# The sixteen-head local attention network: from four-tile rounds to one pipeline over all tiles, with P·V computed transposed

## The chip, the cores and the metric

The kernel runs on one core of a Trainium2 chip. A time is the device time of one execution in microseconds (us). The kernel before took 2250.7, 2259.16 and 2259.73 us in three runs, median 2259.16 us.

## The reference

Two layers run one after the other on x of shape (4, 512, 128): four batches of 512 tokens with 128 features.

```python
x = L0_attn_x
xn = layernorm(x)
s = L0_attn(xn)                 # retention over chunks, 4 heads
g = silu(L0_ffn(xn))            # the network of depth 6, below
x = x + s * g
xn = layernorm(x)
s = L1_attn(xn)                 # one head of masked attention
g = silu(L1_ffn(xn))            # 8 experts, top 2
x = x + s * g
```

The change touches `L0_ffn` alone. Its reference, cut to what matters:

```python
for i in range(6):
    x = attn_layer(shift_tokens(x), Wqkv[i], q_scale[i], k_scale[i], Wo[i]) + x
    x = ffn_layer(shift_tokens(x), ln_g[i], ln_b[i], W1[i], b1[i], W2[i], b2[i]) + x
# attn_layer, 16 heads of 64, windows of 32 tokens:
q, k, v = split(x @ Wqkv)                     # 128 -> 3 * 1024
q, k = l2norm(q) * qs, l2norm(k) * ks         # then rotary, with a scale by position
sim = 8 * q . k  over the own window of 32 and the one before it, masked
out = softmax(sim) @ v, then out @ Wo         # 1024 -> 128
# ffn_layer: layernorm, xn @ W1 + b1 -> a, gate (341 each), a * gelu(gate) @ W2 + b2
```

All is float32.

## The kernel before, in words

Three builders run one after the other: `build_retention`, `build_network` (this is `L0_ffn`, and all that changes) and `build_second_layer`. The features of x lie on the partitions, `state[128, 4 x 516]`.

The network has 6 layers x 4 batches = 24 rounds, and a round has 4 tiles of 128 tokens (96 tiles). For each tile the work is this:

- TensorE projects q and k into `qk_ps` (4 banks, `project_qk` L393) and v into the ring (`project_v` L380). The ring is 2 PSUM banks used in turn by everything that isn't q, k or the scores; before it writes a bank, TensorE waits for the reader of the fill two places earlier (`bank_free`).
- VectorE multiplies q and k by the rotary tables (`rotate` L708, L713; the half `k` after ScalarE's squares), GpSimd adds the two products (L352). ScalarE squares q and k (L575), VectorE sums by head (L721), ScalarE takes Ln and Exp (L580, L584), VectorE makes one Newton step (L733 to L737), and GpSimd multiplies by the inverse norms (L359).
- TensorE transposes q and k (`transpose_qk` L404), ScalarE copies them to SBUF (the helper at L564 makes all such copies). The scores are 64 small matmuls per tile (L423), after two that write the mask (L418), into the two banks `sc_ps`.
- VectorE takes the row maximum (L742), subtracts it (L747), ScalarE exponentiates (L613), VectorE sums the rows (L755) and takes the reciprocal; TensorE transposes exp(S) (L438), ScalarE copies, and TensorE multiplies by the windows of v (`attend` L453) into the same `sc_ps`. VectorE multiplies the product by 1/sum (`normalise` L767), TensorE transposes it (`transpose_o` L467) and ScalarE copies it to `oT`.
- SyncE moves v from token order into windows with 16 DMAs a tile (`move_windows`, L293 and L296).

A tile takes three stages: projections in its own, scores one later, softmax and P·V two later. Once a round come the output projection (L475, 8 matmuls of 512 columns), the LayerNorm (L481, L486), the gated network (L493, L495, `gelu` L603, L789) and its second matrix (L502, L796), all for the round before. The orders are written out by hand for each engine (`pe_round`, `act_round`, `dve_round`): stages s=0 and s=1 of a round hold only tile work, s=2 also the whole output projection and the LayerNorm, s=3 also the whole feed-forward part. Each engine executes its own list strictly in order.

`ident`, `ones` and mask constants are made first. At a layer's first round GpSimd rebuilds the rotary tables `rot` (L341), after VectorE has finished with the old ones.

## Time and profile before

| | before |
|---|---|
| median of 3 runs | 2259.16 us |
| the profiled execution: its own time | 2256.97 us |
| its span, from the first to the last instruction | 2255.2 us |
| mean granted TensorE clock | 0.972 |
| matmul instructions on TensorE | 31016 |
| DMA, q1 | 120.64 MB in 83600 packets |

An instruction line of a list by lines reads: line, engine, operation, output<-input, count | busy us in all, mean ns of one | idle time of the engine just before them and what ended it. PE is TensorE, PEld its weight loads, DVE VectorE, ACT ScalarE, POOL GpSimd, SP SyncE. A float32 matmul appears as two MATMUL instructions, a float32 transpose as one. In a timeline the first number is the start, the second the length of the merged piece, which runs to the modelled end of the last matmul; the distance between two starts tells what a piece costs a busy TensorE.

### The profile page before, as it was taken

The page shows a single profiled execution, that of the slowest core. Times are in us where ns is not written, and L with a number is a line of the kernel's source. Part 1 is how long each engine was busy: PE and PEld are TensorE (multiplying, and loading weights), DVE is VectorE, ACT ScalarE, POOL GpSimd, SP SyncE. Part 2 cuts the span into 40 slices and gives each one's busy share as a digit, 9 for nine tenths or more (in the row PEclk, how much of TensorE's full clock was granted, in tenths as well). Part 3 has the DMA queues.
Part 4 walks back from the last instruction along what each step waited for, and adds up shares of the span by engine and source line. Part 5 has one row for each costly group of instructions (what it writes and reads, how often), then busy time and mean ns, then how long its engine had stood idle before and what let it go on. Part 6 is the DMA issues. An engine that isn't in the chain of part 4 may idle for free. (4 is left out here: it accounts for less than half of the span.)

```text
span 2255.2 us, 71087 instructions
## 1 busy us (share of the span) xinstructions
PE 1958.2 (87%) x31016; PEld 1121.9 (50%) x31016; DVE 1561.8 (69%) x2095; ACT 1151.2 (51%) x1934; POOL 863.9 (38%) x427
## 2 busy tenths in 40 slices
PE   6858889889989898989889898899988888986898
PEld 5635455455545544554555454455544545543444
DVE  6648777777767877777777777778777777863443
ACT  4425555554655555455555555555555555553234
POOL 0225444444434534444443444444445444430000
PEclk9979999999999999999999999999999999997788
DMA  1023222223222322222232222232223222221000
GB/s 42 1 72 93 48 54 60 73 58 75 54 46 56 87 66 58 55 51 67 62 79 50 57 57 74 49 75 62 50 56 86 66 49 56 60 52 43 0 9 10
DMA packets 83885, 124.96 MB, mean 55 GB/s; under 512 B 26112, under 2 KB 31880, under 8 KB 82704
## 3 DMA queue, kind: packets, MB, share of 16 engines
q1 hardware_dynamic: 83600, 120.64, 22.2%
q8 instruction: 242, 3.96, 0.8%
q14 instruction: 43, 0.35, 0.1%
HBM read 21.98 MB, written 1.05 MB: 10 GB/s over the span
## 5 line engine op out<-in xcount | busy, mean ns | idle before, releaser
L352 POOL TENSOR_TENSOR t<-t 128x1024 f32<-128x1024 f32 x192 | 453.3, 2361 | 661.4 <-DVE t L713 661.4
L359 POOL TENSOR_TENSOR qkn<-t,rn 128x1024 f32<-128x1024 f32 x192 | 374.2, 1969 | 373.9 <-DVE rn L737 373.9
L393 PE MATMUL qk_ps<-wqkv,state 128*128 128x512 f32 x768 | 396.5, 599 | 11.5 <-DMA wqkv<-in_w_qkv 9.2
L708 DVE TENSOR_TENSOR t<-qk_ps,rot 128x1024 f32<-128x1024 f32 x192 | 234.5, 1222 | 195.4 <-ACT sq L575 135.5
L404 PEld LDWEIGHTS ring<-ident,qkn 128*128 128x128 f32 x1536 | 180.9, 141 | 198.9 <-issue 122.0
L404 PE MATMUL ring<-ident,qkn 128*128 128x128 f32 x1536 | 233.8, 278 | 26.2 <-POOL qkn L359 25.6
L713 DVE TENSOR_TENSOR t<-qk_ps,rot 128x1024 f32<-128x1024 f32 x192 | 233.1, 1214 | 0.0
L721 DVE TENSOR_REDUCE lnsum<-sq 128x16 f32<-128x1024 f32 x192 | 231.8, 1208 | 0.0
L564 ACT COPY prT<-ring 128x512 f32<-128x512 f32 x192 | 113.2, 590 | 217.2 <-PE ring L438 217.2
L575 ACT ACTIVATE sq<-qk_ps 128x1024 f32<-128x1024 f32 x192 | 198.0, 1031 | 39.0 <-PE qk_ps L393 38.0
L564 ACT COPY oT<-ring 128x512 f32<-128x512 f32 x192 | 112.6, 586 | 184.0 <-PE ring L467 184.0
L380 PE MATMUL ring<-wqkv,state 128*128 128x512 f32 x384 | 200.4, 624 | 3.6 <-DMA wqkv<-in_w_qkv 2.7
L423 PE MATMUL sc_ps<-kT,qT 64*32 64x64 f32 x12288 | 170.6, 224 | 23.9 <-issue 23.9
L423 PEld LDWEIGHTS sc_ps<-kT,qT 64*32 64x32 f32 x12288 | 135.9, 105 | 83.1 <-issue 82.8
L475 PE MATMUL ring<-oT,wo 128*128 128x512 f32 x384 | 170.7, 598 | 0.7 <-ACT oT L564 0.7
L453 PE MATMUL sc_ps<-v_win,prT 64*32 64x64 f32 x12288 | 168.1, 225 | 2.7 <-issue 1.6
L564 ACT COPY v_tok<-ring 128x512 f32<-128x512 f32 x192 | 112.1, 584 | 113.3 <-PE ring L380 113.3
L453 PEld LDWEIGHTS sc_ps<-v_win,prT 64*32 64x32 f32 x12288 | 135.6, 106 | 63.9 <-issue 62.3
L564 ACT COPY qT<-ring 128x512 f32<-128x512 f32 x192 | 111.4, 580 | 104.7 <-PE ring L404 104.7
L742 DVE TENSOR_REDUCE smax<-sc_ps 128x16 f32<-128x1024 f32 x96 | 117.2, 1221 | 68.1 <-PE sc_ps L423 68.1
L438 PE MATMUL ring<-ident,pexp 128*128 128x128 f32 x768 | 120.0, 279 | 29.5 <-ACT pexp L613 20.4
L438 PEld LDWEIGHTS ring<-ident,pexp 128*128 128x128 f32 x768 | 87.8, 140 | 111.0 <-issue 74.7
(235 smaller groups left out, 2727.2 us busy)
## 6 DMA issues: line engine op xcount, KB each, us to landing
v_win<-v_tok SPq DMA_DIRECT2D x1488, 64.0 KB, 2.0
wqkv<-in_w_qkv SPq DMA_DIRECT2D x6, 1024.0 KB, 5.6
wqkv<-in_w_qkv SPq DMA_DIRECT2D x6, 512.0 KB, 3.7
wo<-in_w_o SPq DMA_DIRECT2D x6, 512.0 KB, 3.8
w<-in_w SPq DMA_DIRECT2D x6, 341.0 KB, 4.0
w<-in_w SPq DMA_DIRECT2D x6, 192.0 KB, 3.9
r_xtok<-in_x SPq DMA_DIRECT2D x4, 256.0 KB, 4.0
amask<-in_att_mask SPq DMA_DIRECT2D x1, 1024.0 KB
```

Source lines behind the costliest of these rows:

```text
L352: nc.gpsimd.tensor_tensor(t1[:, to], t1[:, to], t2[:, to], ALU.add).then_inc(qk_added.sem, 1)
L359: nc.gpsimd.tensor_tensor(qkn[:, to].rearrange("p (h d) -> p h d", d=DH), t1[:, to].rearrange("p (h d) -> p h d", d=DH), rn[:, HEADS * hal ...
L380: nc.tensor.matmul(to, tile_of(r, s), wqkv[:, 2 * INNER + 512 * par:2 * INNER + 512 * (par + 1)], start=True, stop=True).then_inc(v_full.s ...
L393: nc.tensor.matmul(qk_ps[:, c, :], tile_of(r, s), wqkv[:, 512 * c:512 * (c + 1)], start=True, stop=True).then_inc(qk_full.sem, 1)
L404: ins = nc.tensor.transpose(to[:, n * P:(n + 1) * P], qkn[:, c * P:(c + 1) * P], ident[:, :])
L423: ins = nc.tensor.matmul(sc_ps[WIN * q:WIN * (q + 1), par, 64 * pair:64 * (pair + 1)], qT[64 * par:64 * (par + 1), pair, WIN * q:WIN * (q ...
L438: ins = nc.tensor.transpose(to[:, n * P:(n + 1) * P], pe_[:, c * P:(c + 1) * P], ident[:, :])
L453: ins = nc.tensor.matmul(sc_ps[WIN * q:WIN * (q + 1), par, DH * pair:DH * (pair + 1)], prT[64 * par:64 * (par + 1), pair, WIN * q:WIN * (q ...
L564: nc.scalar.copy(to, bank_of(r, (what, s, lag, f))).then_inc(done.sem, 1)
L708: nc.vector.tensor_tensor(t1[:, to].rearrange("p (h d) -> p h d", d=DH), own, rot[:, 2 * half, s:s + 1, :].to_broadcast([P, HEADS, DH]), A ...
L713: nc.vector.tensor_tensor(t2[:, to].rearrange("p (h s d) -> p h s d", s=2, d=DH // 2), swapped, rot[:, 2 * half + 1, s:s + 1, :].to_broadc ...
L721: nc.vector.tensor_reduce(lnsum[:, HEADS * half:HEADS * (half + 1)], sq[:, INNER * half:INNER * (half + 1)].rearrange("p (h d) -> p h d", ...
```

## The change

The network is written anew as a single chain of 102 stages (96 tiles and 6 to run empty), in which stage g works on tile g (projections), g-1 (transposes of q and k, scores), g-2 (softmax, transposes of P) and g-3 (P·V). All loops are unrolled, GpSimd's and SyncE's too.

- **P·V transposed.** `attend` makes the windows of v the stationary operand (64 rows x 64 columns) and P the moving one (32 columns), so that the product comes out as `oT` needs it. It goes to the two ring banks, no longer to `sc_ps`, and ScalarE copies it (`copy_o`). The eight transposes of the product and `o_tok` are gone. v and P are ordered so that heads n and n+8 share a chunk.
- **P normalised on GpSimd.** 1/sum is multiplied into exp(S) before the transposes (`scale_p`, two instructions of 128x512), in place of VectorE's `normalise`.
- **GpSimd's order.** q and k are scaled in four quarters of 128x512 in place of two halves of 128x1024, a stage later than they are summed; then come `scale_p` of tile g-2 and the two additions of tile g. The tables of the next layer are made ahead, into a second buffer.
- **The order on VectorE.** A stage begins with the row maximum and, right behind it, the row sum of the same tile (before, the sum stood one stage later). The Newton step stays there, as a maximum and four instructions in place of a maximum and three. On ScalarE a third instruction (a Relu) stands ahead of Ln and Exp, which now come behind the copies of P.
- **The order on ScalarE.** A stage begins with exponential, copy of o, exponential, copy of o.
- **The round's parts are spread.** The output projection is cut in two halves of 256 columns, one in the stage s=1 and one in s=2 of the next round; the LayerNorm is in its s=3, the two matrices of the feed-forward part in s=0 and s=1 of the round after that.
- SyncE loads Wq and Wk in two transfers, Wo at the end of a layer's first round, W1 and W2 in its second round. The moves of v stay as they were.

The diff, cut to its core:

```diff
+def stage_fills(g):
+    now, turn, prob, att = (tile_there(g - n) for n in range(4))
+    up, down = round_at(g, 0, 2), round_at(g, 1, 2)
+    out_0, out_1, centre = round_at(g, 1, 1), round_at(g, 2, 1), round_at(g, 3, 1)
+    fills = []
+    fills += [("a", g - 3, f) for f in range(2)] * att
+    fills += [("xc", centre, 0)] * (centre is not None)
+    fills += [("t", g - 1, 0)] * turn
+    fills += [("w2", down, 0)] * (down is not None)
+    fills += [("t", g - 1, 1)] * turn
+    fills += [(k, up, 0) for k in ("gate", "lin")] * (up is not None)
+    fills += [("t", g - 1, 2)] * turn
+    fills += [("v", g, 0)] * now
+    fills += [(k, up, 1) for k in ("gate", "lin")] * (up is not None)
+    fills += [("t", g - 1, 3)] * turn
+    fills += [("wo", out_0, 0)] * (out_0 is not None)
+    fills += [("var", centre, 0)] * (centre is not None)
+    fills += [("v", g, 1)] * now
+    fills += [("wo", out_1, 1)] * (out_1 is not None)
+    fills += [(k, up, 2) for k in ("gate", "lin")] * (up is not None)
+    fills += [("p", g - 2, f) for f in range(2)] * prob
+    return fills
...
+    def scale_qk(g, f):
+        if f == 0:
+            pool.wait_ge(rn_ready, g + 1)
+        if f % 2 == 0:
+            added = (q_added, k_added)[f // 2]
+            pool.wait_ge(added, g + 1)
+        nc.gpsimd.tensor_tensor(by_head(quarter(qkn, f)), by_head(quarter(qkn, f)),
+                                rn[:, 8 * f:8 * (f + 1)].unsqueeze(2).to_broadcast([P, 8, DH]), ALU.mult).then_inc(qk_scaled, 1)
+    def add_terms(g, k):
+        turned = (q_rot, k_rot)[k]
+        pool.wait_ge(turned, 2 * (g + 1))
+        if g > 0:
+            pool.wait_ge(qkT_full, 4 * (g - 1) + 2 * (k + 1))
+        nc.gpsimd.tensor_tensor(half(qkn, k), half(t1, k), half(t2, k), ALU.add).then_inc((q_added, k_added)[k], 1)
+    def scale_p(g, f):
+        if f == 0:
+            pool.wait_ge(rden_ready, g + 1)
+            if g > 0:
+                pool.wait_ge(pT_full, 2 * g)
+        nc.gpsimd.tensor_tensor(by_head(quarter(pn, f)), by_head(quarter(pe_, f)),
+                                rden[:, 8 * f:8 * (f + 1)].unsqueeze(2).to_broadcast([P, 8, DH]), ALU.mult).then_inc(p_scaled, 1)
+    tables(0)
+    for g in range(TILE_COUNT + 2):
+        if tile_there(g - 1):
+            for f in range(4):
+                scale_qk(g - 1, f)
+        if tile_there(g - 2):
+            for f in range(2):
+                scale_p(g - 2, f)
+        if tile_there(g):
+            for k in range(2):
+                add_terms(g, k)
+        l = g // (B * TILES)
+        if g % (B * TILES) == 2 and l + 1 < DEPTH:
+            tables(l + 1)
...
+    def attend(g, f):
+        t = g % TILES
+        to = [bank_of("a", g, part) for part in range(2)]
         if f == 0:
+            pe.wait_ge(pT_copied, 2 * (g + 1))
+            pe.wait_ge(v_moved[t], moves_of[t] * (g // TILES + 1))
+            for part in range(2):
+                ring_bank("a", g, part)
+        for pair in range(2 * f, 2 * (f + 1)):
             for q in range(TW):
                 for par in range(2):
+                    n = 2 * pair + par
+                    for part in range(2):
+                        ins = nc.tensor.matmul(
+                            to[part][64 * par:64 * (par + 1), P * pair + WIN * q:P * pair + WIN * (q + 1)],
+                            v_win[64 * part:64 * (part + 1), TW * t + q, DH * n:DH * (n + 1)],
+                            prT[64 * part:64 * (part + 1), n, WIN * q:WIN * (q + 1)],
+                            start=True, stop=True)
         if f == 1:
+            ins.then_inc(av_full, 1)
...
+    for g in range(STAGES):
+        now, turn, prob, att = (tile_there(g - n) for n in range(4))
+        up, down = round_at(g, 0, 2), round_at(g, 1, 2)
+        out_0, out_1, centre = round_at(g, 1, 1), round_at(g, 2, 1), round_at(g, 3, 1)
+        for f in range(2):
+            if att:
+                attend(g - 3, f)
+            if now:
+                project_q(g, f)
+        if centre is not None:
+            ffn_centre(centre)
+        if turn:
+            transpose_qk(g - 1, 0)
+        if down is not None:
+            ffn_down(down)
+        if now:
+            project_k(g, 0)
+        if turn:
+            transpose_qk(g - 1, 1)
+        if now:
+            project_k(g, 1)
+        if up is not None:
+            ffn_up(up, 0)
+        if turn:
+            transpose_qk(g - 1, 2)
+        if now:
+            project_v(g, 0)
+        if up is not None:
+            ffn_up(up, 1)
+        if turn:
+            transpose_qk(g - 1, 3)
+        if out_0 is not None:
+            output_projection(out_0, 0)
+        if centre is not None:
+            ffn_variance(centre)
+        if now:
+            project_v(g, 1)
+        if out_1 is not None:
+            output_projection(out_1, 1)
+        if up is not None:
+            ffn_up(up, 2)
+        for f in range(2):
+            if prob:
+                transpose_p(g - 2, f)
+            if turn:
+                scores(g - 1, f)
...
+    def copy_o(g, f):
+        act.wait_ge(av_full, g + 1)
+        t = g % TILES
+        nc.scalar.copy(oT[:, 4 * f:4 * f + 4, P * t:P * (t + 1)], bank_of("a", g, f)).then_inc(oT_copied, 1)
+    def exponentials(g, f):
...
+    def inverse_norms(g):
+        act.wait_ge(sums_ready, 2 * (g + 1))
+        nc.scalar.activation(raised[:, :], sums[:, :], ACT.Relu, bias=low_col[:, 0:1]).then_inc(raised_ready, 1)
+        act.wait_ge(raised_ready, g + 1)
+        nc.scalar.activation(lnss[:, :], raised[:, :], ACT.Ln, scale=LN_SCALE, bias=low_col[:, 1:2]).then_inc(ln_ready, 1)
+        act.wait_ge(ln_ready, g + 1)
+        if g > 0:
+            act.wait_ge(rn_ready, g)
+        nc.scalar.activation(rs[:, :], lnss[:, :], ACT.Exp, scale=-0.5).then_inc(rs_ready, 1)
...
+    for g in range(STAGES):
+        now, turn, prob, att = (tile_there(g - n) for n in range(4))
+        up, centre = round_at(g, 0, 2), round_at(g, 3, 1)
+        for f in range(2):
+            if prob:
+                exponentials(g - 2, f)
+            if att:
+                copy_o(g - 3, f)
+        if centre is not None:
+            centred(centre)
+        for f in range(2):
+            if turn:
+                copy_qkT(g - 1, f)
+        if now:
+            squares(g, 1)
+        if up is not None:
+            gelu(up, 0)
+        if turn:
+            copy_qkT(g - 1, 2)
+        if now:
+            copy_v(g, 0)
+        if up is not None:
+            gelu(up, 1)
+        if turn:
+            copy_qkT(g - 1, 3)
+        if now:
+            squares(g, 0)
+        if centre is not None:
+            inverse_deviation(centre)
+        if now:
+            copy_v(g, 1)
+        if up is not None:
+            gelu(up, 2)
+            nc.scalar.preload_act_table_set(LN_EXP_SET)
+        for f in range(2):
+            if prob:
+                copy_pT(g - 2, f)
+        if now:
+            inverse_norms(g)
...
+    def row_sum(g):
+        dve.wait_ge(exp_ready, 2 * (g + 1))
+        nc.vector.tensor_reduce(den[:, :], by_head(pe_[:, :]), AX.X, ALU.add).then_inc(den_ready, 1)
+        dve.wait_ge(den_ready, g + 1)
+        if g > 0:
+            dve.wait_ge(p_scaled, 2 * g)
+        nc.vector.reciprocal(rden[:, :], den[:, :]).then_inc(rden_ready, 1)
...
+    def inverse_norms(g):
+        dve.wait_ge(sums_ready, 2 * (g + 1))
+        nc.vector.tensor_scalar(ss[:, :], sums[:, :], NORM_FLOOR, None, ALU.max).then_inc(newton, 1)
+        dve.wait_ge(rs_ready, g + 1)
+        nc.vector.tensor_tensor(nw1[:, :], rs[:, :], rs[:, :], ALU.mult).then_inc(newton, 1)
+        dve.wait_ge(newton, 4 * g + 2)
+        nc.vector.tensor_tensor(nw2[:, :], nw1[:, :], ss[:, :], ALU.mult).then_inc(newton, 1)
+        dve.wait_ge(newton, 4 * g + 3)
+        nc.vector.tensor_scalar(nw3[:, :], nw2[:, :], -0.5 * LN_SCALE * LN_SCALE ** 0.5, 1.5 * LN_SCALE ** 0.5, ALU.mult, ALU.add).then_inc(newton, 1)
+        dve.wait_ge(newton, 4 * g + 4)
+        if g > 0:
+            dve.wait_ge(qk_scaled, 4 * g)
+        nc.vector.tensor_tensor(rn[:, :], nw3[:, :], rs[:, :], ALU.mult).then_inc(rn_ready, 1)
...
+    def add_attention(r, f):
+        dve.wait_ge(wo_full, 2 * r + f + 1)
+        if f == 0 and r > 0:
+            dve.wait_ge(xc_full, r)
+            dve.wait_ge(x_ffn, 2 * r)
         for late, rows in enumerate(HALVES):
+            nc.vector.tensor_tensor(xa[rows, 2 * P * f + late:2 * P * (f + 1) + late], bank_of("wo", r, f)[rows, 0:2 * P],
+                                    state[rows, batch_cols(r, 2 * P * f + late, 2 * P)], ALU.add).then_inc(x_attn, 1)
...
+    for g in range(STAGES):
+        now, turn, prob, att = (tile_there(g - n) for n in range(4))
+        up, down = round_at(g, 0, 2), round_at(g, 1, 2)
+        out_0, out_1, centre = round_at(g, 1, 1), round_at(g, 2, 1), round_at(g, 3, 1)
+        if prob:
+            row_max(g - 2)
+            row_sum(g - 2)
+        if now:
+            rotate(g, 0)
+        if up is not None:
+            ffn_gated(up, 0)
+        if down is not None:
+            add_ffn(down)
+        if now:
+            rotate(g, 1)
+        if up is not None:
+            ffn_gated(up, 1)
+        if now:
+            sum_squares(g, 1)
+            sum_squares(g, 0)
+        if up is not None:
+            ffn_gated(up, 2)
+        if out_0 is not None:
+            add_attention(out_0, 0)
+        if out_1 is not None:
+            add_attention(out_1, 1)
+        if now:
+            inverse_norms(g)
+        if centre is not None:
+            ffn_norm(centre)
```

## Rows read from the trace of the kernel before

**Rows 1.** the page, part 1: busy us (share of the span) xinstructions

```profile
PE 1958.2 (87%) x31016; PEld 1121.9 (50%) x31016; DVE 1561.8 (69%) x2095; ACT 1151.2 (51%) x1934; POOL 863.9 (38%) x427
```

**Rows 2.** timeline of PE, a plain stage: start, us, engine, line, operation

```profile
1089.69 1.02 PE L393 MATMUL qk_ps<-wqkv,state 128*128 128x512 f32 x2 [0.86 <-issue]
1090.55 0.60 PE L404 MATMUL ring<-ident,qkn 128*128 128x128 f32 x4
...
1095.53 0.86 PE L453 MATMUL sc_ps<-v_win,prT 64*32 64x64 f32 x64
...
1101.14 0.59 PE L418 MATMUL sc_ps<-mask_bf,ident_bf 128*128 128x512 bf16 x2 [1.46 <-DVE o_tok L767]
...
1104.42 1.02 PE L393 MATMUL qk_ps<-wqkv,state 128*128 128x512 f32 x2
```

**Rows 3.** timeline of PE, the first projections of the network and of round 1

```profile
141.82 6.53 PE L393 MATMUL qk_ps<-wqkv,state 128*128 128x512 f32 x8 [9.23 <-DMA wqkv<-in_w_qkv]
...
201.59 1.02 PE L393 MATMUL qk_ps<-wqkv,state 128*128 128x512 f32 x2
```

**Rows 4.** timeline of PE, output projection, second matrix, start of the next round

```profile
1027.67 7.03 PE L475 MATMUL ring<-oT,wo 128*128 128x512 f32 x16
...
1067.26 2.82 PE L502 MATMUL ring<-gel,w 128*128 128x512 f32 x6
...
1152.80 1.02 PE L393 MATMUL qk_ps<-wqkv,state 128*128 128x512 f32 x2
```

**Rows 5.** timeline of PE, behind the last tile's scores

```profile
2023.27 0.60 PE L404 MATMUL ring<-ident,qkn 128*128 128x128 f32 x4
...
2039.34 2.05 PE L453 MATMUL sc_ps<-v_win,prT 64*32 64x64 f32 x128 [0.68 <-ACT prT L564]
```

**Rows 6.** PE in stretches: us, PE busy (x), PEclk, DMA share, GB/s

```profile
2039.30:2041.40 2.10, 2.05 (x128) 0.50 0.03 8
```

**Rows 7.** timeline of PE, 64 moving columns with full weights (retention)

```profile
93.48 3.68 PE L1061 MATMUL pd<-vsb,at 128*128 128x64 f32 x32
```

**Rows 8.** the last additions (L796): ns min/median/max, first to last start

```profile
L796 DVE SCALAR_TENSOR_TENSOR state<-ring,col,xa x48: 734/750/760, 278.2 to 2073.9; 64x512 f32<-64x512 f32 x48
```

**Rows 9.** GpSimd's product by the inverse norms, by its line

```profile
L359 POOL TENSOR_TENSOR qkn<-t,rn x192: 1899/1902/2284, 156.4 to 2022.5; 128x1024 f32<-128x1024 f32 x192
```

**Rows 10.** groups by line and shape

```profile
L767 DVE TENSOR_TENSOR o_tok<-sc_ps,rden 128x512 f32<-128x512 f32 x192 | 122.9, 682 | 5.1 <-PE sc_ps L453 4.8 <-issue 0.3
...
L564 ACT COPY oT<-ring 128x512 f32<-128x512 f32 x192 | 112.6, 586 | 184.0 <-PE ring L467 184.0
L613 ACT ACTIVATE pexp<-pr 128x512 f32<-128x512 f32 x192 | 112.6, 628 | 18.5 <-DVE pr L747 18.4
...
L783 DVE TENSOR_SCALAR xn<-xc,col 128x512 f32<-128x512 f32 x24 | 46.7, 1946 | 0.9
...
L341 POOL TENSOR_TENSOR rot<-rot_base,qks 128x256 f32<-128x256 f32 x24 | 16.7, 729 | 10.2 <-DMA qks<-in_qk_scale 10.2
...
L1694 DVE TENSOR_SCALAR apr<-aex,arden 128x512 f32<-128x512 f32 x16 | 7.8, 486 | 0.6
```

**Rows 11.** timeline of DVE, the start of a plain stage

```profile
1088.28 1.23 DVE L742 TENSOR_REDUCE smax<-sc_ps 128x16 f32<-128x1024 f32 x1 [0.41 <-PE sc_ps L423]
1089.54 1.29 DVE L747 TENSOR_TENSOR pr<-sc_ps,smax 128x512 f32<-128x512 f32 x2
```

**Rows 12.** timeline of ACT, squares and gelu of stage s=3

```profile
1058.30 1.05 ACT L575 ACTIVATE sq<-qk_ps 128x1024 f32<-128x1024 f32 x1
1059.37 1.28 ACT L603 ACT_TABLE_LOAD   x1
```

**Rows 13.** timeline of ACT and DVE, Ln to the Newton step

```profile
1022.67 0.23 ACT L580 ACTIVATE lnss<-ss 128x32 f32<-128x32 f32 x1 [2.07 <-DVE ss L726]
...
1023.65 0.19 DVE L737 SCALAR_TENSOR_TENSOR rn<-nw,rs 128x32 f32<-128x32 f32 x1
```

**Rows 14.** what SP waited for: us in total, times, longest us

```profile
SPq L293 <- ACT v_tok L564: 815.7, 96, 15.7
```

804 lines of the change are left out of this document (284 added, 520 removed).

## The prediction

> **What bounds the kernel now.** I read the engines' busy shares first [rows 1]: TensorE is busy for 87% of the span, and nothing else is above 69%, so the question is what TensorE waits for. The share is an average, so next come the stretches between rounds. The network starts its first projection at 141.8 and round 1 at 201.6 [rows 3]; the transposes behind the last scores of round 23 start at 2023.3 [rows 5], and the last addition to the state ends at 2074.6 (2073.9 and 0.75) [rows 8]. Round 0 is thus 59.8 us, 23 rounds take 1821.7, or 79.2 each, and the emptying 51. The other 322 us of the span are untouched code.
>
> Within a round I read TensorE's timeline. A plain stage (s=1) takes 14.7 us, and near its end TensorE stands 1.46 us at the mask matmul, until VectorE has normalised the product of P and V out of the banks that the scores need [rows 2]; with the tail of the matmul before, some 1.7 us are lost, and 13.0 are work. The two stages with round work, s=2 and s=3, take 48.4 us together (1104.42 to 1152.80) [rows 2, 4]. Four times 13.0 plus the round's own matmuls, some 17 (6.9 for the output projection and 2.7 for the second matrix by [rows 4], six up-matmuls and the two of the LayerNorm at 0.9), are 69 of the 79.2: ten microseconds a round are waits.
>
> **What the change takes from TensorE.** The transposes of the product go: two groups of four, 0.60 each with a tail [rows 2], about 1.0 us a stage. P·V has as many matmuls as before, 64 a tile and two instructions each, but 64 stationary columns for 32 and 32 moving ones for 64. Its price isn't in the trace. Now 64 instructions pass in 0.86 [rows 2]. At half clock [rows 6] 128 pass in 2.05 [rows 5], only a fifth more than two such pieces: so at full clock it isn't the array that sets their pace, and the array alone could go nearly twice as fast. Twice the weights then about fill the pace they have: I take 0.85 a half, 1.7 a tile. From the other side, 32 matmuls with 128 stationary and 64 moving columns pass in 3.68 us, 0.11 each [rows 7]; half the columns would be 0.055, or 7.0 us a tile one behind the other and 3.5 if the two halves of the partitions load side by side. Both are kept for the range, and so is 0.8 a tile, should the halved moving columns count. TensorE's own work is then 12.1 a plain stage and 65 to 66 a round.
>
> The Trainium skill ("TensorE: Matmul & The Clock Gate", LDWEIGHTS) speaks against the edit: it counts a load by its columns, at 1.2 columns a ns, so that 64 take 53 ns where 32 took 27. By it P·V would be 3.4 a tile with two loads side by side. The trace agrees for the full weights of the retention, and 32 columns two abreast would take the 0.86 of now; but if that rate falls with the array's clock, the half-clock piece would have taken 3.4 us and not 2.05.
>
> **What takes the old wait's place.** The scores no longer wait for VectorE's normalising; `sc_ps` is free. But in the new order I find another chain. Let a plain stage start at 0 on TensorE, when the scores of tile g-2 are done.
> - VectorE isn't there yet: ScalarE's Ln and Exp now stand behind the two copies of P, whose second transpose ends 0.9 before the stage does. The copy is 0.59 [rows 10], Relu, Ln and Exp 0.75 (0.23 and a gap each), and the Newton step 0.95, where now three instructions and two waits lead from 1022.67 to 1023.84 together with Ln and Exp [rows 13]. So the row maximum starts at 1.6.
> - It takes 1.26 to the first subtraction (0.68) [rows 11]; then the exponential (0.63) and, queued behind it, the first copy of o (0.59) [rows 10]: done at 4.8. Only then is the ring bank free for the first transpose of q. TensorE has by then done P·V and two projections, 3.4 by my price, and stands about 1.4. Even at 3.5 a tile for P·V it would lose only a further 0.4.
> - From there: four transposes at 0.45, two k and two v projections at 0.86 to 0.95, P and the scores (mask 0.5, two halves at 0.8), with one stop of 0.9 where ScalarE has the squares of k (1.05 [rows 12]) ahead of the copies. The stage closes at 14.1, against 14.7 now.
>
> VectorE has some 12 of work there: the row maximum, the subtractions [rows 11], seven more passes over 1024 elements of that length, the reciprocal and the Newton step. The change takes 1.4 from it with `normalise` (two of 0.682 [rows 10]) and adds 0.2 in the Newton step. Nothing is gained by that alone, since VectorE now waits for the exponentials (1.1) and the norms (0.7).
>
> GpSimd: four quarter products at 1.05 and two for P at 1.05, between half of 1.90 [rows 9] and what a line from 0.73 for 256 elements [rows 10] to 1.90 for 1024 gives for 512. That is 6.3 and the two additions' 4.7, 11.0 of 14.1. The reciprocal is there at 7, the two P quarters at 9.2, and TensorE asks for the first at 10.8: hidden, up to some 1.8 for a quarter.
>
> The moves of v: SyncE waited 815.7 us in 96 waits for the copies of v [rows 14], 8.5 a tile; the product reads the windows a stage later than now. Hidden, and the weight loads too. The tables made ahead save the table wait at layer boundaries, under 3 us each; this I leave in the average.
>
> **Stages with round work**, walked in the same way:
> - s=3 (LayerNorm): two more fills and a copy and a square on ScalarE ahead of the copies of q: 16.6. VectorE ends with the normalisation of x, behind the Newton step. The scaling there (L783) is 1.95 now, beside GpSimd's product of 1.90, though one of the same size and kind alone takes 0.49 [rows 9, 10]. It waited out the GpSimd instruction. Quarters make that about 1.1. VectorE comes to the next stage at 3.2.
> - s=0 (gate and linear, six fills): the first transpose of q is held to 6.4 by that lag; then each second fill waits for a gelu or for VectorE's product: the table load (1.28) and the first gelu behind the squares hold the third transpose by 2.3, the gated product the v projection, ScalarE's squares of q the last linear part. 22.9, where the matmuls are 17.9.
> - s=1 (second matrix, half the output projection): the third transpose waits 0.8 for VectorE's addition to the state, the first of P 0.2 for the half just projected: 20.5.
> - s=2 (the other half): 17.5.
>
> Together 77.5, and 0.4 for semaphores: 77.9 against 79.2. The time of a round hardly moves, since the two-bank ring and strict queues give the waits back in other places.
>
> The Trainium skill ("SBUF — State Buffer", "SBUF: two separate sides") says that GpSimd and VectorE hold one pair of ports by turns, also against a VectorE operation with two SBUF inputs. The 1.95 of L783 agrees. By it three of the four Newton instructions, with two such inputs each, could stand behind a GpSimd one. GpSimd waits for the Newton result itself at that point, so the sum would be the same, except where the second addition is late: then up to 2.4 a stage.
>
> **The sum**, against the profiled execution's 2257.0 (span 2255.2 and 1.8 around it; the median, 2259.2, is 0.1% above):
> - round 0: stages of 10, 13, 14 and 14 and no round work, 51 for 59.8: -9
> - round 1: 14.1, 17.7, 17.5 and 16.7, still without the feed-forward part, 66 for 79.2: -13
> - 22 rounds at -1.3: -29
> - emptying: six stages, 20.6 and 11 with work of tiles, then P·V, projection, LayerNorm and the two matrices with nothing beside them, 28: 60 for 51: +9
> - stops not seen in a walk (instruction supply: the 0.86 "issue" in [rows 2], which is in the 79.2): half a microsecond a round: +12
>
> 2257 - 30 = **2227 us**.
>
> **The rivals.**
> 1. Fewer waits: s=0 and s=1 come down to near the matmuls, because the queues drift apart less than in my walk. 65.5 of TensorE work a round allow it; the ten waits of now speak against. At 74 a round: 2227 - 22 x 3.9 = 2141.
> 2. Slower, by the ring: in s=0 some fourteen fills pass through two banks whose readers, ScalarE and VectorE, each have squares, sums or a table load ahead of the read. If each handover there and in s=1 costs 0.2 more than I count, that is 4 us more a round. For: in s=2 and s=3 now 5 of 48.4 us are lost in the same kind of handovers; against: this is already as much as my walk has. At 82 a round: 2227 + 22 x 4.1 = 2317. It decides the sign from 79.3 a round on.
> 3. The weight loads bound P·V: at 3.5 a tile about +1.3 a round, 2256; at 7.0, one behind the other, TensorE is 3.9 late at the transpose in three stages of four: +13 a round, 2515.
> 4. The change doesn't do what it says: P's normalising isn't off the path, because a quarter on GpSimd takes as long as a half does now, 1.9. Six of them put the first P quarter at 11.1, 0.3 late in three stages of four: +1 a round, 2249.
>
> **Chances.** Forecast 0.45, rival 1 0.20, rival 2 0.24, rival 3 0.08, rival 4 0.03. A change under 0.5% (11 us) can't be told from none. The forecast's own range, 2200 to 2255, gives 0.38 faster and 0.07 same; rival 3 gives 0.05 same and 0.03 slower, rival 4 0.03 same. Faster 0.58, same 0.15, slower 0.27. The range runs from a little under rival 1 to rival 2: 2130 to 2320.
>
> **What would show it.** TensorE's wait at the mask for VectorE gone; in its place one at the first transpose of q for ScalarE's copy of o, 1 to 1.5 us a stage and more in s=0; P·V 64 instructions in about 0.85; stages of 14, 17.5, 20.5, 23 and 16.6; L783's successor near 1.1; GpSimd near 1070 us busy (863.9 now [rows 1]). It is wrong if P·V pieces take over 1.2 us, if the P transposes wait for GpSimd, or if a round is under 75 or over 80.

## The result, and the profile after

| | before | after |
|---|---|---|
| median in the comparison (6 runs each) | 2259.4 us | 2270.3 us |
| lowest and highest | 2250.7, 2266.4 | 2267.4, 2275.7 |
| ratio after/before, 95% interval | | 1.0053, 1.0029 to 1.0077 |
| span of the profiled execution | 2255.2 us | 2267.6 us |
| mean granted TensorE clock | 0.972 | 0.968 |

The change made the kernel slower by 0.5%, where 2227 us, faster, was forecast. The time lies inside the range given, on the other side of no change.

The 11 us between the medians may be the granted clock's alone. The profiled executions have 0.972 before and 0.968 after, and the six of the kernel after lie between 0.964 and 0.969. From 200 to 2000 us the kernel before has no stretch at the lower of the two levels (1.2 GHz), and the kernel after has five, 27 us together with a granted clock of 0.50. Each begins within 1.3 us behind a wait of TensorE of 1.4 to 2.2 us: three stops inside P·V, two waits for the copy of o. At most half of the 27 us, some 14, can be lost by them (an estimate from the two levels). Executions of one kernel differ in the same way: `norms`, below, took 2222 us at a clock of 0.974 and 2243 at 0.966. No run holds the clock fixed, so small differences between kernels are to be read with that in mind.

The busy shares of the kernel after, to be read against [rows 1]:

```profile
PE 1959.0 (86%) x30532; PEld 1194.3 (53%) x30632; DVE 1444.6 (64%) x2044; ACT 1177.7 (52%) x2030; POOL 1086.5 (48%) x811
```

TensorE's busy share went from 87 to 86% and its busy time didn't fall, although eight transposes a stage are gone. VectorE gave up work, ScalarE is nearly where it was, and GpSimd's 1086.5 us is near the 1070 of the prediction. Next, twenty rounds each, from the first projection of round 2 to that of round 22. First before, then after; the columns are window, its length, busy time of each engine (with instructions), granted clock, DMA share, GB/s:

```profile
280.93:1865.30 1584.37, 1418.60 (x24923) 796.89 (x24922) 1174.88 (x1541) 858.51 (x1461) 704.09 (x341) 1.00 0.26 62
```

```profile
265.26:1867.69 1602.43, 1421.23 (x24528) 857.59 (x24601) 1076.21 (x1504) 880.61 (x1540) 886.97 (x657) 0.99 0.25 61
```

A round takes 80.1 us against 79.2. TensorE is busy for 71.1 us of it, against 70.9: that is the main finding of this view, since the prediction has 65 to 66 of work. Its idle time is 9.1 against 8.3. Some of the groups behind these sums, TensorE's lines in the same windows, before and then after (line, operation, operands, count, busy us and mean ns, idle before it and what ended it):

```profile
L393 PE MATMUL qk_ps<-wqkv,state 128*128 128x512 f32 x641 | 328.2, 594 | 0.9 <-issue 0.9
...
L453 PE MATMUL sc_ps<-v_win,prT 64*32 64x64 f32 x10240 | 139.6, 224 | 1.6 <-issue 1.4
L467 PE MATMUL ring<-ident,o_tok 128*128 128x128 f32 x642 | 105.5, 286 | 1.1 <-issue 1.1
```

```profile
L427 PE MATMUL ring<-prT,v_win 64*64 64x32 f32 x10247 | 202.3, 222 | 53.9 <-issue 53.7
L379 PE MATMUL ring<-ident,qkn 128*128 128x128 f32 x1280 | 197.9, 277 | 74.0 <-ACT gel L596 29.7 <-ACT kT L542 23.1 <-ACT oT L525 19.4
L357 PE MATMUL qk_ps<-wqkv,state 128*128 128x512 f32 x321 | 186.3, 663 | 1.3 <-issue 1.3
...
L366 PE MATMUL qk_ps<-wqkv,state 128*128 128x512 f32 x320 | 166.1, 601 | 0.0
```

The transposes of the product (L467) were 105.5 us. P·V went from 139.6 (L453) to 202.3 (L427), up 62.7. The projections of q and k, 328.2 in L393, are 352.4 in L357 and L366, up 24.2: each pair now stands between other work and carries a tail. The output projection in halves of 256 columns is up 7.1 (140.6 to 147.7). So 94.0 of the 105.5 are given back. These are busy times with modelled ends, so a part of them is tails. From one start to the next, a projection of two instructions right behind a half of P·V takes 1.06 us (below, 1093.16 to 1094.22), where 0.86 was usual before ([rows 2], 1089.69 to 1090.55). The wait at the mask for VectorE that [rows 2] show once, 67.2 us in this window before, is gone as predicted. In its place are 53.7 us of "issue" inside P·V (time in which TensorE waited for nothing that the profile shows), where before there were 1.4, and more waiting at the transposes of q and k (74.0; before, L404 had 15.7).

The order on TensorE at a stage boundary, in a timeline (start, length, operation, idle before and releaser):

```profile
1091.24 0.86 PE L396 MATMUL sc_ps<-kT,qT 64*32 64x64 f32 x64
1092.08 1.15 PE L427 MATMUL ring<-prT,v_win 64*64 64x32 f32 x64
1093.16 1.13 PE L357 MATMUL qk_ps<-wqkv,state 128*128 128x512 f32 x2
...
1096.81 0.63 PE L379 MATMUL ring<-ident,qkn 128*128 128x128 f32 x4 [0.40 <-POOL qkn L299]
```

A piece of 64 instructions of P·V occupies 1.08 us up to the next start (1092.08 to 1093.16), where the prediction had 0.85; the same number for the scores, 1091.24 to 1092.08, takes 0.84. The transposes at 1096.81 waited 0.40 us, and the view puts that down to GpSimd's scaled q. GpSimd's own line shows that it was another:

```profile
1093.75 4.05 POOL L299 TENSOR_TENSOR qkn<-qkn,rn 128x512 f32<-128x512 f32 x4 [5.58 <-DVE rn L721]
```

The first of its four quarters, all that the first transposes read, was done at 1094.8, two microseconds earlier. What ended at 1096.67, 0.1 us before the load of their weights, is ScalarE's first copy of o (its line stands below), which holds the bank of the ring that they write. An example of a stop in the same group, some 80 us before:

```profile
1013.41 0.90 PE L427 MATMUL ring<-prT,v_win 64*64 64x32 f32 x48
1015.13 0.43 PE L427 MATMUL ring<-prT,v_win 64*64 64x32 f32 x16 [0.81 <-issue]
```

And VectorE around that boundary (the scores end at 1011.3):

```profile
1008.47 0.17 DVE L710 TENSOR_SCALAR ss<-sums 128x32 f32<-128x32 f32 x1
1011.65 0.19 DVE L712 TENSOR_TENSOR nw<-rs 128x32 f32<-128x32 f32 x1 [3.02 <-ACT rs L575]
...
1012.43 1.22 DVE L657 TENSOR_REDUCE smax<-sc_ps 128x16 f32<-128x1024 f32 x1
```

VectorE has the sums ready at 1008.6, waits 3.02 us for ScalarE's Exp, and starts the row maximum at 1012.43, 1.1 after the scores' last matmul. The mean of this lag over all stages, from the modelled end of the last score matmul to the start of the maximum, is 1.73 us, against 0.54 before. ScalarE, at the boundary of the timeline further up:

```profile
1091.35 0.59 ACT L553 COPY prT<-ring 128x512 f32<-128x512 f32 x1 [0.71 <-PE ring L410]
...
1092.54 0.23 ACT L575 ACTIVATE rs<-lnss 128x32 f32<-128x32 f32 x1
1095.56 0.63 ACT L533 ACTIVATE pexp<-pr 128x512 f32<-128x512 f32 x1 [2.79 <-DVE pr L664]
1096.10 0.57 ACT L525 COPY oT<-ring 128x512 f32<-128x512 f32 x1
```

The Exp of the norms (1092.54) comes last, behind both copies of P, and then ScalarE stands for 2.79 us until VectorE has subtracted. What was waited for in 150 to 2000 us (engine, tile and line, what ended the wait: us in total, times, longest):

```profile
DVE nw L712 <- ACT rs L575: 268.1, 93, 3.9
...
PEld ring L379 <- POOL qkn L299: 83.2, 78, 5.3
...
PE ring L427 <- issue: 57.8, 74, 1.7
...
PE ring L379 <- ACT oT L525: 22.8, 19, 2.2
...
PE sc_ps L396 <- issue: 17.6, 27, 1.3
```

PEld is the queue of the weight loads, which runs ahead of the matmuls: its 83.2 us aren't TensorE standing still, and from round 2 on they weren't for GpSimd either. In the trace the quarter that a load reads had been done for 2.0 us or more before each load of these transposes in those rounds; of the 86 first loads of a stage, 82 start within 0.15 us behind the end of a copy of o. So the matmuls' own line, 22.8 us for the copy of o, is the one to read. All of it falls in 19 of the 22 stages s=0:

```profile
666.73 0.57 ACT L525 COPY oT<-ring 128x512 f32<-128x512 f32 x1
```

```profile
667.44 0.63 PE L379 MATMUL ring<-ident,qkn 128*128 128x128 f32 x4 [2.05 <-ACT oT L525]
```

Stops with nothing to wait for inside P·V and the scores sum to 75 us in this stretch, against 26 before (23.9 in the scores, 1.6 in P·V).

Stages of a round, from one tile's first projection to the next, are 23.6, 21.5, 17.8 and 17.1 us for s=0 to 3 (means from round 2 on): 80.0. Round 0 takes 59.2 us, as against 59.8 in [rows 3], and round 1 65.4; the emptying, from the end of the last stage with projections (2023.4) to the end of the last addition (2084.3), takes 61 (51 by [rows 5, 8]). In round 0 GpSimd does hold the matmuls, in three stages (TensorE's waits from 140 to 200 us):

```profile
PE ring L379 <- POOL qkn L299: 8.0, 3, 4.5
```

Two groups of the page answer to [rows 9]:

```profile
L299 POOL TENSOR_TENSOR qkn<-qkn,rn 128x512 f32<-128x512 f32 x384 | 401.4, 1076 | 461.5 <-DVE rn L721 461.5
...
L316 POOL TENSOR_TENSOR pn<-pexp,rden 128x512 f32<-128x512 f32 x192 | 196.4, 1044 | 185.2 <-DVE rden L676 153.9
```

The successor of L783 [rows 10], L739, has a mean of 1.12 us.

### The profile page after: what moved, and what is told of

The parts are those of the page before. It is cut to its first block and busy times, and to the rows that moved or that the text cites. A ratio compares the mean times of both kernels' runs of the same rounds, so it can differ in the third digit from the quotient of the medians.

```text
span 2267.6 us, 70947 instructions
## 1 busy us (share of the span) xinstructions
PE 1959.0 (86%) x30532; PEld 1194.3 (53%) x30632; DVE 1444.6 (64%) x2044; ACT 1177.7 (52%) x2030; POOL 1086.5 (48%) x811
## 3 DMA queue, kind: packets, MB, share of 16 engines
q8 instruction: 240, 3.93, 0.8%
HBM read 21.98 MB, written 1.05 MB: 10 GB/s over the span
## 5 line engine op out<-in xcount | busy, mean ns | idle before, releaser
L299 POOL TENSOR_TENSOR qkn<-qkn,rn 128x512 f32<-128x512 f32 x384 | 401.4, 1076 | 461.5 <-DVE rn L721 461.5
L308 POOL TENSOR_TENSOR qkn<-t 128x1024 f32<-128x1024 f32 x192 | 452.2, 2362 | 193.6 <-PE ring L379 116.5
L427 PE MATMUL ring<-prT,v_win 64*64 64x32 f32 x12288 | 240.8, 222 | 62.1 <-issue 61.1
L427 PEld LDWEIGHTS ring<-prT,v_win 64*64 64x64 f32 x12288 | 213.3, 136 | 154.1 <-issue 142.4
L316 POOL TENSOR_TENSOR pn<-pexp,rden 128x512 f32<-128x512 f32 x192 | 196.4, 1044 | 185.2 <-DVE rden L676 153.9
L533 ACT ACTIVATE pexp<-pr 128x512 f32<-128x512 f32 x192 | 121.3, 632 | 315.0 <-DVE pr L664 315.0
L691 DVE TENSOR_TENSOR t<-qk_ps,rot 128x1024 f32<-128x1024 f32 x192 | 228.7, 1191 | 65.4 <-ACT sq L563 57.4
L357 PE MATMUL qk_ps<-wqkv,state 128*128 128x512 f32 x384 | 222.5, 664 | 12.9 <-DMA wqkv<-in_w_qkv 7.4
L705 DVE TENSOR_REDUCE sums<-sq 128x16 f32<-128x1024 f32 x192 | 226.3, 1211 | 3.4 <-ACT sq L563 3.1
L671 DVE TENSOR_REDUCE den<-pexp 128x16 f32<-128x1024 f32 x96 | 117.1, 1220 | 144.3 <-ACT pexp L533 144.3
L366 PE MATMUL qk_ps<-wqkv,state 128*128 128x512 f32 x384 | 201.5, 607 | 0.0
L396 PE MATMUL sc_ps<-kT,qT 64*32 64x64 f32 x12288 | 172.2, 224 | 17.9 <-issue 17.8
L442 PE MATMUL ring<-oT,wo 128*128 128x256 f32 x768 | 177.1, 384 | 1.2 <-ACT oT L525 1.2
```

Of the source, the lines that this page charges most:

```text
L299: nc.gpsimd.tensor_tensor(by_head(quarter(qkn, f)), by_head(quarter(qkn, f)), rn[:, 8 * f:8 * (f + 1)].unsqueeze(2).to_broadcast([P, 8, DH ...
L308: nc.gpsimd.tensor_tensor(half(qkn, k), half(t1, k), half(t2, k), ALU.add).then_inc((q_added, k_added)[k], 1)
L357: nc.tensor.matmul(qk_ps[:, f, :], tile_of(g), quarter(wqkv, f), start=True, stop=True).then_inc(q_full, 1)
L366: nc.tensor.matmul(qk_ps[:, 2 + f, :], tile_of(g), quarter(wqkv, 2 + f), start=True, stop=True).then_inc(k_full, 1)
L396: ins = nc.tensor.matmul(sc_ps[WIN * q:WIN * (q + 1), par, 64 * pair:64 * (pair + 1)], qT[64 * par:64 * (par + 1), pair, WIN * q:WIN * (q ...
L427: ins = nc.tensor.matmul(to[part][64 * par:64 * (par + 1), P * pair + WIN * q:P * pair + WIN * (q + 1)], v_win[64 * part:64 * (part + 1), ...
```

## The experiments

Four theories were kept apart. A: TensorE starves for instructions, because scores and P·V now stand back to back. B: the 64x64 form of P·V is dear. C: VectorE comes late to each stage, through the norms that ScalarE makes behind its copies of P, and that chain sets the stage. D, the prediction's own: the copy of o, queued behind the exponential, holds the first transpose of q. C and D aren't rivals all the way: the chain from VectorE's late row maximum through the exponential ends at the copy of o. Times are medians of 4 to 10 runs; a ratio is to the kernel before, run beside it on the same chip (in the five comparisons its median is 2256.7 to 2259.8 us, so times of different comparisons can be set side by side). Four kernels don't compute the reference: `shape` and `norms_shape` leave out the transposition of the product, `half_pv` and `norms_half_pv` half of P·V.

| kernel | us | ratio, 95% interval |
|---|---|---|
| after | 2270.3 | 1.0053, 1.0029 to 1.0077 |
| `spaced` | 2282.4 | 1.0122, 1.0090 to 1.0153 |
| `shape` | 2260.4 | 1.0012, 0.9993 to 1.0031 |
| `norms` | 2236.3 | 0.9895, 0.9859 to 0.9930 |
| `p_on_vector` | 2303.6 | 1.0204, 1.0179 to 1.0229 |
| `norms_shape` | 2216.6 | 0.9826, 0.9807 to 0.9844 |
| `norms_sum` | 2234.6 | 0.9924, 0.9893 to 0.9955 |
| `half_pv` | 2245.2 | 0.9952, 0.9936 to 0.9969 |
| `spaced_norms` | 2274.4 | 1.0074, 1.0054 to 1.0094 |
| `norms_first` | 2239.3 | 0.9893, 0.9852 to 0.9934 |
| `norms_exp` | 2231.3 | 0.9866, 0.9828 to 0.9904 |
| `norms_half_pv` | 2159.1 | 0.9552, 0.9518 to 0.9585 |
| `norms_q_ahead` | 2241.2 | 0.9916, 0.9893 to 0.9938 |

**`spaced`** puts projections between the bursts of short matmuls.

```diff
+ project_q(g, 0); project_q(g, 1)
  attend(g - 3, 0)
- project_q(g, 0)
+ project_k(g, 0)
  attend(g - 3, 1)
- project_q(g, 1)
+ project_k(g, 1)
... (the two calls of project_k further down go)
```

> The changed kernel, with the two q projections ahead of both halves of P.V and the k projections between and behind them, so that 128 pairs of small matmuls and loads (scores, second half) are no longer followed at once by 64 more (P.V, first half). No instruction is added or left out. Theory A (TensorE runs out of instructions where such bursts stand back to back; the stops inside one group were 61.1 us at P.V and 17.8 at the scores, against 23.9 at the scores and 1.6 at P.V before): the stops at P.V fall to a third, some 40 us less in all, 2230 us. Theory B (the 64x64 form of P.V itself is slow, and stops come from it): stops and time stay within 10 us of 2270. Theory C (the order of VectorE and ScalarE and the two-bank ring set the stage): o is copied 0.9 us later and the transposes of q start later, so 2270 to 2300.

```profile
PE ring L379 <- DVE state L751: 32.1, 22, 1.5
...
PE sc_ps L396 <- issue: 14.1, 21, 1.2
```

The stops inside a group fell from 75 to 14 us, and the time rose by 12, as theory C had it and against A. Other waits of TensorE rose by 48 us in their place (the sum of its waits is 207 in the kernel after and 194 here), among them 32.1 for VectorE's addition to the state. Taking the stops away by this order gains nothing.

**`shape`** gives P·V the operands of the kernel before (P stationary, v moving); the product isn't transposed, so the copy of o takes it as it is.

```diff
- to[part][64 * par:64 * (par + 1), P * pair + WIN * q:...], v_win[..., DH * n:...], prT[..., n, WIN * q:...]
+ to[part][WIN * q:WIN * (q + 1), DH * n:DH * (n + 1)], prT[..., n, WIN * q:...], v_win[..., DH * n:...]
```

> The changed kernel, with P.V computed in the form of before: P stationary (64 rows x 32 columns), the windows of v moving (64 columns), as many matmuls, into the same ring banks. The product then lies in token order and isn't turned, so the rest computes with the wrong numbers: what is left out is the transposition of the product. Theory B (the form costs): a piece of 64 takes 0.79 us again instead of 1.07, 0.56 a stage, 96 stages: up to -54 us, 2216, if nothing else holds the stage. Theory C (the stage is held by row maximum, exponential, copy of o, first transpose of q): the wait of that transpose for the copy of o comes up in most stages, from 24 us to over 80, and the gain is under 20 us. Theory A: the stops at P.V stay, since instructions are used up even faster; time 2240 to 2260.

```profile
1084.32 1.01 PE L427 MATMUL ring<-v_win,prT 64*32 64x64 f32 x64
1085.26 1.13 PE L357 MATMUL qk_ps<-wqkv,state 128*128 128x512 f32 x2
```

It gained 10 us (2260; its interval and that of the kernel after just touch), under the 20 of theory C. The wait for the copy of o didn't grow as that theory had it: 23.1 us against 22.8. A half of P·V takes 0.94 us to the next start, for 1.07 in the kernel after and 0.79 in the kernel before (medians of the halves without a stop). So the form makes 0.12 of the rise of 0.28; the rest comes with where P·V now stands or writes, and no run tells which. The stops inside P·V grew from 57.8 to 72.8 us in its trace: some of what the faster form gives is taken by them.

**`norms`** moves three small instructions on ScalarE by one place.

```diff
- copy_pT(g - 2, 0); copy_pT(g - 2, 1)
- inverse_norms(g)
+ copy_pT(g - 2, 0)
+ inverse_norms(g)
+ copy_pT(g - 2, 1)
```

> The changed kernel, with ScalarE's Relu, Ln and Exp for the norms between the two copies of P in place of behind both. Theory C (VectorE comes 1.6 us late to each stage because it waits for the norms; it stood 273 us in 95 waits for them): the wait falls by 1 us a stage, the exponentials and the copy of o come earlier, 20 to 60 us less, 2210 to 2250. Theories A and B: the copy of o isn't what TensorE waits for (24 us in all), so the time stays within 8 us, or is a little longer where the norms hold the second copy of P up (P.V then waits for it).

```profile
DVE nw L713 <- ACT rs L575: 127.0, 96, 2.1
...
PE ring L427 <- issue: 60.9, 69, 1.6
...
DVE smax L658 <- PE sc_ps L396: 32.8, 53, 1.6
...
PE ring L379 <- ACT oT L525: 2.7, 6, 0.6
```

It gained 34 us, with the stops in P·V as they were (60.9). VectorE's wait for the norms fell from 268 to 127 us, its mean lag behind the scores from 1.73 to 0.48, and it now waits for the scores (32.8) instead of coming late to them. That is theory C. Where the lag had held TensorE is theory D's place: the wait for the copy of o fell from 22.8 to 2.7, stage s=0 from 23.6 to 22.4 us, and in it the first transpose of q starts 5.4 us behind the start of P·V in place of 6.5 (means from round 2 on). The other stages together changed by 0.1 us. Some 20 of the 34 us are that one wait.

**`p_on_vector`** takes `scale_p` from GpSimd and has VectorE do the same two products behind the reciprocal.

```diff
# GpSimd
- scale_p(g - 2, 0); scale_p(g - 2, 1)
# VectorE, end of row_sum(g)
+ ... (waits for the reciprocal and for pn to be free)
+ for f in range(2):
+     nc.vector.tensor_tensor(by_head(quarter(pn, f)), by_head(quarter(pe_, f)), rden[...], ALU.mult)
```

> The changed kernel, with 1/sum multiplied into exp(S) on VectorE, right behind the reciprocal (two instructions of 128x512), in place of GpSimd. It undoes the part of the change that moved the normalising to GpSimd. Theory C: VectorE's chain gets 1.3 us longer and comes late: stages with round work longer by up to 1.3, +30 to +100 us. Theories A and B: VectorE has 2.9 us of waiting for the norms in a stage to take it from, and P was never late on GpSimd: within 12 us of 2270. If the GpSimd form had been what delays the stages, it would be faster by more than 20.

It lost 33 us. Two products of 0.69 us more on VectorE, some 130 us in all, cost a quarter of their length: VectorE's time is on the path, in part of the stages.

**`norms_shape`** joins the edits of `norms` and `shape`.

> The Relu, Ln and Exp of the norms between ScalarE's two copies of P, and P.V in the form of the kernel before (64x32 stationary, 64 columns moving), the product not transposed. Alone the first gave 2236 us (34 below the changed kernel) and the second 2260 (10 below). Theory C (VectorE's lag sets the stage): with the lag mostly gone TensorE is nearer to the end of the stage, so what the form costs (0.25 to 0.3 us a half, 2 halves in 96 stages, 50 us of TensorE) shows more than before: 2236 less 10 to 35, 2200 to 2226 us. Theory B (the form costs about 10 us whatever else bounds): 2226. Theory A (the supply of instructions is the bound, and the form changes no count): 2236 within 5.

With the norms early the form is worth 20 us (2236 to 2217), about twice what it is in the kernel after, as theory C had it; 0.12 us for each of 192 halves is 23.

**`norms_sum`** is `norms` with `row_sum(g - 2)` behind `rotate(g, 0)` on VectorE.

```diff
- row_max(g - 2); row_sum(g - 2); rotate(g, 0)
+ row_max(g - 2); rotate(g, 0); row_sum(g - 2)
```

> The norms between the two copies of P, and on VectorE the row sums and the reciprocal after the q half's rotation instead of ahead of it. In the changed kernel VectorE waits 144 us (1.5 a stage) at the row sum for ScalarE's exponentials; the two products of the rotation can be done in that time, if q's projection is there. Theory C: VectorE gets up to 1 us a stage earlier through its stage, and with it the norms and the products on GpSimd: 2236 less 20 to 60, 2176 to 2216 us. Theory A: TensorE's stops stay and fill what is won, 2236 within 10. A rival within C: P comes later from GpSimd (scaled after the sum), TensorE waits at the transposes of P, and the time is 2236 to 2260.

2235: no gain over `norms`, though the 230 us of waiting at the row sum are gone; theory C had 20 to 60 us, theory A at most 10. TensorE's idle time from 150 to 2000 us is 198.7 in its trace, 197.6 in `norms`. Past `norms`, this order of VectorE's no longer counts.

**`half_pv`** and **`norms_half_pv`** issue 64 of the 128 matmul instructions of a stage's P·V, on the kernel after and on `norms`.

```diff
- for part in range(2):
+ for part in (par,):
      ins = nc.tensor.matmul(to[part][...
```

> Leaves out half of P.V: of the 128 matmuls of a stage's product only 64 are issued (one of the two banks for each parity), everything else as in the changed kernel. It takes 1.1 us a stage from TensorE, 106 us in all, and about half of the 61 us of stops in that group. Theories A and B (TensorE with its stops is the end of the stage): 2270 less 100 to 150, 2120 to 2170 us. Theory C (VectorE's lag and the hand-overs with ScalarE set most stages): TensorE waits longer at the transposes of q and k instead, and less than half of it shows: 2210 to 2255 us.

> Half of P.V left out (64 of 128 matmuls a stage) as in half_pv, with the norms between the two copies of P. In the changed kernel leaving it out gave only 25 of the 106 us of TensorE's time (and none of the stops), and TensorE waited 147 us for the scaled q and k instead. Theory C: with the norms early that wait has room, TensorE is nearer to the bound, and more of it shows: 2236 less 50 to 110, 2126 to 2186 us. If something else holds the stage than the lag through the norms: 2236 less 10 to 35, 2200 to 2226.

Both expectations took it that half the matmuls are half the time on TensorE. They aren't. TensorE's timeline of `half_pv`:

```profile
1121.80 1.12 PE L427 MATMUL ring<-prT,v_win 64*64 64x32 f32 x32
1122.86 1.12 PE L357 MATMUL qk_ps<-wqkv,state 128*128 128x512 f32 x2
```

32 instructions take 1.06 us to the next start, where 64 took 1.08. That two neighbours with different halves of the rows had gone side by side is a guess: what is left out also changes which quarter of the array follows which. P·V's busy time in twenty rounds falls only from 202.3 to 184.0 us. What the edit mainly takes away is instructions: 48 of the 240 packets of the instruction queue, and with them most stops. Part 3 of the page, in the kernel after and in `half_pv`, and the waits of `half_pv` and of `norms_half_pv`:

```profile
q8 instruction: 240, 3.93, 0.8%
```

```profile
q8 instruction: 192, 3.15, 0.6%
```

```profile
DVE nw L712 <- ACT rs L575: 273.7, 95, 3.9
...
PE ring L379 <- ACT oT L525: 40.1, 21, 2.2
...
PE ring L427 <- issue: 10.2, 17, 1.1
```

```profile
PE ring L427 <- issue: 12.4, 20, 1.3
...
PE ring L379 <- ACT oT L525: 8.6, 13, 2.0
```

So this pair takes the stops away with every order left as it is. Stops inside a group fell from 75 to 23 us in the one and from 81 to 22 in the other. Both times lie where theory C had them (2245 and 2159), the first far from A's and B's 2120 to 2170. The edit is worth 25 us in the kernel after and 77 with the norms early; the norms are worth 34 us with the stops and 86 without most of them.

With the norms early the sum comes out: 58 us fewer stops and 19 less busy time of P·V in twenty rounds (202.1 to 182.8) are 77. In the kernel after, 52 and 18 are 70, and only 25 show. What came in their place is in the trace: TensorE's wait for the copy of o rose from 22.8 to 40.1 us, in 21 of 22 stages s=0, behind a VectorE that waits for the norms as long as ever (273.7); the same copy holds the LayerNorm's first matmul for 10.6 us in place of 3.3. And the granted clock was lower: 0.958 to 0.964 in its four executions, 0.964 to 0.969 in those of the kernel after. From 200 to 2000 us its trace has 58 us at the lower level for 27, which can hide up to 15 us more. The expectation of `norms_half_pv` speaks of 147 us of waiting for the scaled q and k; 129 of them are the weight loads' line, put down to the wrong engine. Neither A nor C is the cause alone: taking one away shows in full only once the other is gone.

**`spaced_norms`** joins the edits of `spaced` and `norms`.

> The spaced order of TensorE (both projections of q ahead, then a half of P.V, k 0, the other half, k 1) together with the norms between the two copies of P. Spaced alone was 2282 with the stops inside a group down from 76 to 15 us. Theory A and C together (stops were hidden behind VectorE's lag): with the lag gone the missing stops count, and it comes to lie below norms alone: 2190 to 2230 us. Theory C alone: the spaced order starts P.V later and so the copy of o and everything behind it on ScalarE: 2236 to 2260, as much over norms alone (2236) as spaced was over the changed kernel (12).

It lost 38 us against `norms`, more than spacing lost against the kernel after and outside both ranges. So the spaced order has a cost of its own, larger than the stops it avoids; the trace again has 32.1 us of waiting for the addition to the state, and the rest wasn't taken apart.

**`norms_first`** has the norms ahead of both copies of P.

```diff
- copy_pT(g - 2, 0); copy_pT(g - 2, 1); inverse_norms(g)
+ inverse_norms(g); copy_pT(g - 2, 0); copy_pT(g - 2, 1)
```

> The Relu, Ln and Exp of the norms ahead of both of ScalarE's copies of P (norms: between the two, 2236 us). With the norms between the copies VectorE still waits 127 us for the Exp, ScalarE itself 94 us for the transposes of P. Theory C: the 127 us nearly vanish, the copies of P come 1 us later at most, since ScalarE was waiting for P anyway: 2236 less 5 to 25, 2211 to 2231 us. If by now TensorE is the end of the stage (its stops and its own work): 2236 within 6, and the wait before P.V grows.

2239, the same as `norms` within their spread. VectorE's wait for the norms fell again, from 127 to 75 us, and nothing came of it: theory C's further 5 to 25 us aren't there. ScalarE's order behind P offers no more.

**`norms_exp`** asks about theory D: on `norms`, both exponentials stand ahead of both copies of o.

```diff
- exponentials(g - 2, 0); copy_o(g - 3, 0); exponentials(g - 2, 1); copy_o(g - 3, 1)
+ exponentials(g - 2, 0); exponentials(g - 2, 1); copy_o(g - 3, 0); copy_o(g - 3, 1)
```

> Norms between the copies of P, and on ScalarE both exponentials ahead of both copies of o (before: exponential, copy of o, exponential, copy of o). The row sums on VectorE can start a copy earlier (0.6 us a stage of the 230 us that they wait in norms), while the two banks of the ring come free later for the first two transposes of q. Theory C: if VectorE's lag still counts, 2236 less 10 to 40. If the hand-over of the ring counts, as the prediction had it (1 to 1.5 us a stage behind the first copy of o): 2236 plus 30 to 70. If TensorE is the end by its own work: within 8 of 2236.

```profile
PE ring L427 <- issue: 59.2, 75, 1.7
...
PE ring L379 <- ACT oT L525: 7.1, 10, 1.2
```

The first copy of o comes an exponential later, and TensorE waits for it 7.1 us in all. The time is 5 us below `norms`, inside both spreads. With the norms early, the copy of o had room. That says nothing of the kernel after, where it had none in 19 of 22 stages s=0.

**`norms_q_ahead`** is `norms_exp` with each half of q's projection ahead of its half of P·V.

```diff
- attend(g - 3, 0); project_q(g, 0); attend(g - 3, 1); project_q(g, 1)
+ project_q(g, 0); attend(g - 3, 0); project_q(g, 1); attend(g - 3, 1)
```

> norms_exp (norms between the copies of P, both exponentials ahead of both copies of o; 2231 us), and on TensorE each half of q's projection ahead of its half of P.V instead of behind it (q 0, P.V 0, q 1, P.V 1). One projection of 0.54 us then stands between the 64 short matmuls of the scores and the first 64 of P.V; the copy of o comes one projection later, not three as in the spaced order. Theory A on top of C (TensorE is the bound now, so its stops inside a group, 79 us, count): the stops fall to 30 to 50 us and the time by 15 to 40, to 2191 to 2216 us. Theory C alone (the stops come back elsewhere, or the later copy of o costs as much): 2225 to 2250.

```profile
PE ring L379 <- ACT oT L525: 61.6, 70, 2.1
...
PE ring L427 <- issue: 6.5, 19, 0.5
```

The stops in P·V fell from 59.2 to 6.5 us, and the wait for the copy of o rose from 7.1 to 61.6: a projection's delay was more than the room it had. The median is 10 us above that of `norms_exp`, with intervals that overlap. Together with `spaced` and `spaced_norms`, an order that removes stops cost what it gained or more, three times out of three; of the edits that removed stops, only the one with fewer instructions gained.

The best kernels that compute the reference are `norms_exp`, `norms_sum` and `norms`, at 2231, 2235 and 2236 us, within each other's spread: 1.3, 0.8 and 1.1% below before by the ratios, 1.5 to 1.7% below the kernel after.

## Why the prediction was wrong

The step that failed is the price of TensorE's own work: 65 to 66 us a round, with P·V at 0.85 a half and stops at half a microsecond a round. The runs show 71.1 us busy a round, 1.08 a half, and 3.3 us of stops a round (75 us in 23 rounds). The chain that the walk put in the old wait's place is there, about as long as it was worked out.

The sum missed by 43 us. Its own terms, by the trace: round 0 took 59.2 us for 51, +8; 22 rounds took 79.9 us each for 78.4 (77.9 and the half microsecond of stops), +33; round 1 (65.4 for 66), the emptying (61 for 60) and the start (140.6 for 141.8) came out as worked out; the untouched code behind the last addition took 183.3 us for 180.6, +3. Up to 14 us of the 33 can be the five stretches of lower clock, which no term had. Step by step:

- **The stops of instruction supply, +12 us: wrong by far, and the largest measured part of the miss on TensorE.** Inside groups they rose from 26 to 75 us. The prediction took half a microsecond a round from a single stop of its plain stage; it didn't see that the new order ends a stage on the second half of the scores and begins the next with P·V, 128 instructions one behind the other, which before had other work between them. Taken away, together with half of P·V's matmuls, they are worth 25 us here and 77 with the norms early.
- **P·V at 0.85 a half: wrong.** It took 1.08. The step argued that the array doesn't set the pace, since half the clock slowed a piece by only a fifth, and that twice the weights then cost nothing. 0.23 over two halves of 80 tiles are 37 us in twenty rounds of TensorE's time. The 0.86 that it started from was a length with its tail; from start to start a half took 0.79 before. Less than half of the rise is the form: `shape` has 0.94, and undoing it gave 10 us in the kernel after, 20 with the norms early. The Trainium skill ("TensorE: Matmul & The Clock Gate", LDWEIGHTS) counts a load at 1.2 columns a ns, by which 64 columns cost 53 ns, an estimate from that page. The trace has 17 ns for each load with its matmul (1.08 us for 64), and 33 in `half_pv` (1.06 us for 32): that more columns are dearer holds, the size doesn't.
- **TensorE's own work of 12.1 in a plain stage, 65 to 66 a round: wrong.** Busy for 71.1 us a round, it saved nothing against 70.9. The transposes' 5.3 us a round went into P·V (3.1), projections cut by other work (1.2) and the halved output projection (0.4). The walk had 0.86 to 0.95 for each projection, and those right behind P·V take 1.06.
- **VectorE starts a stage 1.6 late, because Ln and Exp stand behind P's copies: right.** 1.73 on average.
- **The lag then holds the first transpose of q through the exponential and the copy of o: right, and its size right where TensorE gets there early.** In s=0 the walk had the first transpose held to 6.4; it starts at 6.5, with waits of 1.2 us on average in 19 of 22 stages. In a plain stage the walk had it at 4.8 with 1.4 of standing; in s=1 it starts at 5.1 with next to no standing, because TensorE's own work up to there, 3.4 by the walk, takes 4.3 (1092.08 to 1096.4 in the timeline) and more where a stop falls in. So the wait of 1 to 1.5 us a stage is 22.8 us in all: the dearer work stands in its place. Taking the lag away (`norms`) gives 34 us, and the walk had that cost in it.
- **Round 0 at 51: wrong, 59.2.** The walk had stages of 10, 13, 14 and 14; TensorE waits 8.0 us at the first transposes of its last three for GpSimd's scaled q. The first instruction of VectorE there waits 7.8 us for the rotary tables, for which GpSimd waited 9.6 for the loaded scales.
- **The wait at the mask gone: right.** So were **GpSimd's quarters** (1.08 and 1.04 us for 1.05), its P products off the path (`p_on_vector` prices that move at 33 us in favour of the change), and L783's successor: 1.12 us for about 1.1, from 1.95.
- **Stages:** 23.6, 21.5, 17.8 and 17.1 for 22.9, 20.5, 17.5 and 16.6. The longest miss is s=1, then s=0.
- **Rivals.** Rival 2, the ring's handovers from 79.3 a round on, has the right sign, and s=0 and s=1 miss most, as it had it, by 1.7 us of its 4. What `norms` takes away is one such handover, the bank that the copy of o holds; the others weren't varied, so how much of the miss is theirs stays open. Rival 3 (weight loads bound P·V at 3.5 a tile): a tile takes 2.16, and loads half as wide (`shape`) make it 1.9; that the loads are what bounds it is likely and not shown. Rival 4 is refuted; the transposes of P waited for GpSimd once in the whole run, for 0.7 us. Rival 1 is refuted for the kernel after; its 74 a round is under the 74.4 that TensorE is busy for and stops.

Why the whole was slower: two chains are nearly equally long, and the change lengthened both. TensorE's got back, in P·V, in projections and in stops, all that the transposes had cost; VectorE's round trip through ScalarE's norms left it 1.2 us a stage later than before (1.73 for 0.54), and with it the copy of o. Shortening either gives 10 to 34 us; the norms and half of P·V's matmuls together, most stops with them, gave 111 (2270.3 to 2159.1). So the 43 us can't be split over the steps: each term's worth depends on the others. The form and the norms undone together bring it to 2216.6, 11 below the forecast, without touching the stops. That the change lost 0.5% rather than nothing may be the clock.

What stays open: what the lower clock cost, since it also follows from waits and was never held fixed; the 0.16 us a half of P·V that isn't its form; and the last step from instruction packets to stops, since only their number was changed and not their speed.

## What to carry to other kernels

When two chains are about equally long, taking work from one gives a fraction of it, so an edit's worth is best measured again after the other chain has been shortened. Where a view names who ended a wait, check that engine's own timeline before building on it: here the product named had been done for two microseconds, and the true releaser was the copy beside it. Small instructions that end a long queue (here a Relu, an Ln and an Exp of 128x32, 0.9 us together) deserve the earliest place their inputs allow: what follows them on other engines can weigh more than the copy they delay (34 us here). Where an order puts bursts of many short matmuls next to each other (here 128 instructions and more), count the instructions as well as their time: stops for their supply are part of the sum.

## What the runs showed of the hardware

- The 64x64 form with 32 moving columns passes at 17 ns an instruction with its load (1.08 us for 64). In the same place the 64x32 form with 64 moving columns takes 15 (`shape`, 0.94), and 12 to 13 in the scores and in the P·V of before (0.79 to 0.84). The wider load costs more than the shorter stream saves. Leaving out every second matmul of the 64x64 form saved no time in a burst (1.06 us for 32); whether that is because neighbours passed side by side wasn't tested.
- A projection of two instructions of 128x512 takes 1.06 us to the next start right behind a half of P·V, 0.86 elsewhere.
- Stops of up to 2.1 us with nothing to wait for stand inside dense bursts of such pairs: 77 times in P·V and 28 in the scores over the whole run. They end 1.1 to 1.6 us after a packet of the queue for instructions has landed; the page counts 240 such packets, 3.93 MB. That this supply causes them is inferred from that timing and from `half_pv`, where a fifth fewer packets took away two thirds of them; that density brings them is shown by `spaced` and `norms_q_ahead`, where they fell from 75 to 14 us and from 78 (`norms_exp`) to 24 with the same packets.
- Behind some waits of TensorE of 1.4 to 2.2 us, inside rounds in which it is busy for nine tenths of the time, the granted clock was 0.50 for a few microseconds: five times in the kernel after. In `spaced`, behind an idle time of 1.88 us the granted clock was 0.61 over 4.35 us, and two projections that start 0.86 apart elsewhere took 1.5 to 1.7:

```profile
1003.56 0.63 PE L379 MATMUL ring<-ident,qkn 128*128 128x128 f32 x4 [1.88 <-ACT gel L595]
1004.25 1.71 PE L371 MATMUL ring<-wqkv,state 128*128 128x512 f32 x2
1005.75 1.91 PE L458 MATMUL ring<-xn,w 128*128 128x512 f32 x2
```

```profile
1004.25:1008.60 4.35, 4.35 (x6) 0.61 0.00 0
```
